# Graph attention: the aggregate of units 52 to 55 is issued one round sooner, behind scores 60 and 61

## The reference, cut to what matters

```python
for l in range(L):
    q = ((x @ Wq[l].T + bq[l]) * scaling).reshape(n, H, DH)
    k = (x @ Wk[l].T).reshape(n, H, DH)
    v = (x @ Wv[l].T).reshape(n, H, DH)
    scores = jnp.einsum('ehd,ehd->eh', q[tgt], k[srcidx])
    m = jax.ops.segment_max(scores, tgt, num_segments=n)
    p = jnp.exp(scores - m[tgt])
    s = jax.ops.segment_sum(p, tgt, num_segments=n)
    w = p / (s[tgt] + 1e-16)
    agg = jax.ops.segment_sum(w[:, :, None] * v[srcidx], tgt, num_segments=n)
    attn = agg.reshape(n, D) @ Wo[l].T + bo[l]
    x = _batchnorm(x + attn, g1[l], beta1[l])
    ff = jax.nn.relu(x @ W1[l].T + b1[l]) @ W2[l].T + b2[l]
    x = _batchnorm(x + ff, g2[l], beta2[l])
```

## Time and profile before

| what | value |
|---|---|
| time, median of 3 runs | 1014.09 us (1011.72 to 1014.5) |
| the profiled execution, its own time | 1012.98 us |
| its span, first to last instruction | 1011.2 us |
| TensorE busy (matmul) | 950.0 us, 94% |
| VectorE busy | 623.2 us, 62% |
| ScalarE busy | 494.1 us, 49% |
| GpSimd busy | 251.4 us, 25% |
| mean DMA rate | 95 GB/s |
| mean granted TensorE clock, as a share of full speed | 0.985 |

### The profile page before, as it was taken

One profiled execution on the slowest core, in us unless ns is written; L12 is line 12 of the kernel. 1 busy time (PEld: TensorE's weight loads), 2 busy tenths in 40 slices (PEclk: granted clock), 3 DMA queues, 4 the chain that ended last, 5 costly groups with the idle time before them and its releaser, 6 DMA issues.

```text
span 1011.2 us, 15231 instructions
## 1 busy us (share of the span) xinstructions
PE 950.0 (94%) x5362; PEld 677.3 (67%) x5362; DVE 623.2 (62%) x1087; ACT 494.1 (49%) x767; POOL 251.4 (25%) x138
## 2 busy tenths in 40 slices
PE   6999999999999999999999999999999999999915
PEld 2735545788878786887777777747777776777313
DVE  4676566557777335348776674535576676746395
ACT  1665344554734313227666666213576666641154
POOL 2000000499942051410000047112100000570500
PEclk9999999999999999999999999999999999999978
DMA  9201100000200201236655673111076555722002
GB/s 328 80 0 42 41 1 22 1 1 1 84 1 1 102 24 42 84 125 189 187 181 172 193 226 105 45 39 42 22 210 189 178 173 168 238 75 78 28 0 84
DMA packets 58848, 96.14 MB, mean 95 GB/s; under 512 B 8284, under 2 KB 38172, under 8 KB 58270
## 3 DMA queue, kind: packets, MB, share of 16 engines
q1 hardware_dynamic: 55454, 93.11, 29.2%
q10 hardware_dynamic: 3328, 2.15, 0.7%
HBM read 59.58 MB, written 33.55 MB: 92 GB/s over the span
## 4 chain that ended last, share of the span: by engine, by line
PE 85%; DVE 6%; issue 3%; DMA 2%; ACT 2%; POOL 1%; SPq 0%; DVEq 0%; ACTq 0%
PE slots L1820 75%; PE slots L1904 9%; POOL X L741 1%; DMA W<-in_wkT 1%; DMA PT<-blocks 1%; ACT X L1131 1%; DVE XT L1551 0%; DVE X L1705 0%; POOL WL L721 0%; DVE SM L1682 0%; DVE XT L1572 0%; DVE st L1668 0%; DVE PT L1771 0%; DVE SM L1610 0%; SPq L607 0%
## 5 line engine op out<-in xcount | busy, mean ns | idle before, releaser
L1820 PE MATMUL slots<-PT,XN 128*64 128x256 f32 x1024 | 117.6, 382 | 0.7 <-DMA PT<-blocks 0.6
L1820 PE MATMUL slots<-KS,QS 64*128 64x512 f32 x768 | 107.3, 406 | 5.5 <-DVE nm L1610 5.2
L1610 DVE CUSTOM_DVE_ANT_0 SM<-slots,MASK 128x1024 f32<-128x1024 f32 x64 | 75.7, 1220 | 50.2 <-PE slots L1820 50.2
L1820 PEld LDWEIGHTS slots<-PT,XN 128*64 128x64 f32 x1024 | 72.8, 137 | 42.3 <-issue 12.0
L766 POOL TENSOR_TENSOR QS<-QF,QS 128x512 fp32r<-128x512 f32 x16 | 20.7, 1294 | 319.6 <-ACT QS L1051 319.6
L1820 PEld LDWEIGHTS slots<-KS,QS 64*128 64x128 f32 x768 | 72.8, 184 | 24.3 <-issue 11.3
L1035 ACT ACTIVATE SM<-SM,nm 128x1024 f32<-128x1024 f32 x64 | 73.4, 1147 | 26.5 <-DVE nm L1610 26.5
L813 ACT ACTIVATE PT<-slots 128x1024 f32<-128x1024 f32 x68 | 69.4, 1021 | 33.2 <-PE slots L1904 26.9
L1820 PE MATMUL slots<-PT 128*128 128x512 bf16 (+3 forms) x392 | 77.3, 367 | 2.5 <-ACT PT L813 1.2
L1035 ACT ACTIVATE PT<-PT,nm 128x1024 f32<-128x1024 f32 x64 | 73.4, 1146 | 12.9 <-DVE nm L1610 11.6
L1610 DVE CUSTOM_DVE_ANT_0 PT<-slots,MASK 128x1024 f32<-128x1024 f32 x64 | 75.2, 1212 | 4.1 <-PE slots L1820 4.0
(11 more groups left out here) (403 smaller groups left out, 2150.1 us busy)
## 6 DMA issues: line engine op xcount, KB each, us to landing
blocks<-FL SPq DMA_DIRECT2D x56, 512.0 KB, 3.2
PT<-blocks SPq DMA_DIRECT2D x224, 128.0 KB, 3.5
X<-in_x SPq DMA_DIRECT2D x4, 512.0 KB, 11.6
W<-in_wout SPq DMA_DIRECT2D x2, 1024.0 KB, 6.4
W<-in_gq SPq DMA_DIRECT2D x2, 1024.0 KB, 5.0
W<-in_gk SPq DMA_DIRECT2D x2, 1024.0 KB, 5.3
spill<-X SPq DMA_DIRECT2D x4, 512.0 KB, 2.6
SXR<-XTR SPq DMA_DIRECT2D x1, 2048.0 KB, 8.7
```

The costliest lines, as they stand in the source:

```text
L1610: nc.vector.tensor_tensor_reduce(out=SMs[n % SMB], in0=src, in1=MASK[:, unit(n)[2], :], scale=-1.0, scalar=-0.1 * NO_EDGE, op0=ALU.add, op ...
L1820: return nc.tensor.matmul(o_, lhsT, rhs, start=start, stop=stop)
```

## The change

The step `agg` 13 stands one round sooner in the list: it was issued in the round m = 58, behind the turns of 58 and 59 and scores 62 and 63, and is now issued at m = 56, behind the turns of 56 and 57 and scores 60 and 61. No other step moves, and both layers take the same list.

```diff
@@ attention_order @@
-        if m >= 6 and m % 4 == 2 and m < UNITS - 4:
+        if m >= 6 and m % 4 == 2 and m < UNITS - 8:
             order.append(("agg", m // 4 - 1))
-        if m in (UNITS - 4, UNITS):
+        if m in (UNITS - 8, UNITS - 4, UNITS):
             order.append(("agg", m // 4 - 1))
```

## The result

The changed kernel takes 1016.06 us (median of 20 runs, 1012.39 to 1022.49) against 1013.0 for the kernel before beside it (20 runs): ratio 1.0029, 95% interval 1.0016 to 1.0041, so 3 us slower. The prediction counted from 1014.09, the median of the first three runs, its range went from 1014.4 to 1020.6, and it gave 0.64 to a kernel slower by more than 0.3%: the measured time lies inside the range, and the change is just under that bound. The profiled execution has a span of 1013.8 us, against 1011.2.

The account below looks back on a forecast made before the run. TensorE was taken to bound the kernel. From 1014.09 us, new waits of 4.25 less closed gaps of 1.46 gave +2.8, and one clock fall +1.5: +4.3, so 1018.4 us, range 1014.4 to 1020.6.

Parts of the forecast that it names:

- Closed gap, -1.46 us: Ahead of scores 62 and 63 TensorE waits 0.73 us for DVE to take out score 61; this closes in both layers.
- New waits, 2.33 + 1.92 = 4.25 us: Ahead of aggregate 13, TensorE waits for unit 55's blocks through memory: 2.33 us in the first layer, 1.92 in the second.
- Nothing behind the waiting aggregate held up: Behind aggregate 13, ACT's exponential of 61 is ready 0.2 us before the turn of 61 wants it; nothing added.
- A: The moment of aggregate 13's first matmul, from which the starts of later steps on TensorE and ACT were counted.
- The loss reaches the end: Behind both layers' waits the chain is TensorE-bound, so nothing takes up the 2.79 us.
- The clock falls in one of the two layers, +1.5: Behind the waits at aggregate 13, TensorE's clock drops to 1.2 GHz in one layer, costing 1.5 us; chance 0.5.
- the likeliest case: Both layers wait at aggregate 13 and the clock falls in one: +2.8 + 1.5 = +4.3, 1018.4 us, chance 0.41.
- waits without a fall: Both layers wait at aggregate 13 and the clock holds: +2.8, 1016.9 us, chance 0.28.
- The rival on the other side: At aggregate 13 the fetches land in time and it fills the gap DVE leaves: 1.46 us gained, 1012.6, chance 0.05.
- The transfer cost of a page: For unit 55's fetches: about 2.0 us fixed plus bytes over 436 GB/s, landing after 2.3 us; a gain of 0.5 us.
- The clock rule of a page: TensorE's clock follows how busy it has lately been, with two levels; by it the change pays twice for its waits.

Follow-up runs that it names:

- turn_55: The changed kernel with unit 55 turned by TensorE and no longer carried through memory; ratio 1.0003 to the kernel before.
- agg_between: The kernel before with aggregate 13 only half a round sooner, between the turns of 58 and 59 and scores 62 and 63; ratio 0.9984.
- between_again: Repeat of the kernel before with aggregate 13 between the turns of 58 and 59 and scores 62 and 63; ratio 0.9989.
- fetch53_early: The changed kernel with the fetches of unit 53 issued straight behind its own store, ahead of unit 55's store; ratio 1.0024 to the kernel before.
- change_again: The changed kernel measured a second time, nothing else changed; ratio 1.0034 to the kernel before.

## Why the prediction was right on the wait and not on the clock

- **Closed gap, -1.46 us:** right. Waits for DVE fell by 1.4 us, and the gap is missing in every variant in which the aggregate stands between the two pairs of scores.
- **New waits, 2.33 + 1.92 = 4.25 us:** right in place and cause, a bit long. 2.06 and 1.73 in the profile after, 2.59 and 1.17, 1.98 and 1.05 in the repeats, so 3.53 us on average for both layers. Landings scatter from execution to execution by half a microsecond or more, and the one trace of before had a landing in the second layer that was later than in all three profiles of the changed kernel.
- **Nothing behind the waiting aggregate held up:** right to 0.02 us. ACT's exponential of 61 was forecast at A + 6.60 and came at 615.68 + 6.58; the turns of 60 and 61 at A + 7.08 and came at A + 7.10. turn_55 confirms it from the other side.
- **The loss reaches the end:** right, but 2.35 us at the place against 2.6 in the span is a closer match than the parts: 0.6 us of the span is the fall of the clock near the end, which no sum had.
- **The clock falls in one of the two layers, +1.5:** the term that was too large in its odds. The fall is real and costs 1.58 to 1.69 us when it comes at this place, but in the three profiled executions of the changed kernel, six waits, it came once, some 0.5 us an execution. At aggregate 13 it followed waits of 2.24, 2.59 and 2.67 us and those near 5, and none of 2.06 or less. The sums of the prediction had 2.33 and 1.92, and its odds of even and one in three rested on one fall in one trace. The same trace had a fall at 148.4 with TensorE busy, and the odds did not count it. The medians with and without the extra transposes differ by 1.6 and 1.8 us, but the profiles show no such difference at this place. How much of the loss is the clock, and where, isn't settled.
- **Sum:** +4.3 was forecast for the likeliest case, +2.8 for waits without a fall. Measured: +2.9, +3.4 and +4.0 us. That lies between the two cases, as a mixture of executions with and without a fall would, but the fall near the end adds to it too, so that the sum came out near is in part luck. The forecast of 1018.4 stands a further 1.1 us too high because it counts from the median of three runs: 20 runs of the kernel before gave 1013.0. The rival on the other side, that the aggregate fills the gap, is what agg_between does: it asks 1.9 us later and gains 1.1 to 1.6 us.
- **The transfer cost of a page:** by the Trainium skill ("DMA: Bandwidth & Descriptors", the section on the anatomy of one DMA) a fetch would have landed after an estimated 2.3 us and the change would have gained. The last fetches took 3.0 to 5.0 us in the profiles, so the measurement decides against that figure for these transfers.
- **The clock rule of a page:** the Trainium skill ("TensorE: Matmul & The Clock Gate", section "What's actually happening") says that the clock follows how busy TensorE has lately been. The runs agree in part: at aggregate 13 it fell only behind the longest waits, and it stayed up in the four waits filled with transposes. The fall at 148.4, behind rows that show TensorE busy, doesn't fit that reading of the rows.

## What to carry to other kernels

Before moving a consumer forward on the engine that bounds the kernel, read when its last input lands and compare that with the new moment of asking, not with the old one: here the slack was 2 us and the move took 4.2. The best place was between the two: in a gap that was there anyway and hardly ahead of the landing. And a wait of over 2 us on TensorE can cost 1.6 us more by its clock. Filling such a wait made the kernel faster here in two comparisons out of two, by a way that the profiles don't show, and a fill that lasts longer than the wait costs its excess. Last, a mean clock over the whole span doesn't tell where the clock fell: list the windows.

## What the runs showed of the hardware that had not been expected

- The way of one unit through memory, from the issue of its 512 KB store to the first matmul that uses it, took 7.2 to 9.4 us where TensorE stood waiting for it (the longest in between_again: 889.60 - 880.21 = 9.39), with no difference that these single profiles could show by what else was in the queues; two layers of one execution differed by up to 1.9 us (fetch53_early: 618.42 - 609.23 = 9.19 and 894.52 - 887.28 = 7.24).
- The lower level of the clock can begin in the wait itself: with the 5 us wait the window 610.45 to 615.45 shows 0.73 on average. The work behind it then starts slow.
- A wait of several semaphores is put down to the one that came last by the profile, and at 616.36 in change_again this named DVE. Its event and the landing came within 0.1 us of each other; the profile after, in which the aggregate starts ahead of that event of DVE, and the list of waits in the kernel show that it was the landing.
- Of the four fetches of the last unit through memory the fourth took longest in every layer of every profile: 3.0 to 5.0 us from issue to landing, against 2.4 to 3.6 for the first three. The aggregate needs all four.
- The clock fell behind one and the same idle stretch of 2.14 us in 11 executions and not in 2, and behind an idle stretch of 1.76 us and one of 0.7 near the end in 6 of 13.
